# A new order of all engines' turns in the graph stage of a graph-attention and routed-experts kernel

## The reference

```
n = layernorm(x)
h = n @ W
logits = (h @ a_1)^T + h @ a_2 + (h @ a_12) @ h^T        # 512 x 512 for each graph
e = leaky_relu(logits, 0.2);  e = where(adj > 0, e, -9e15)
x = x + elu(n @ W_1 + (softmax(e) @ n) @ W_2)

r = layernorm(x)
top2 of (r @ gate_w + gate_b), weights by softmax over the two
moe = sum over the two of  weight * (relu(r @ w1[e] + b1[e]) @ w2[e] + b2[e])
x = x + layernorm(r + moe) * gamma + beta
```

## Time and profile before

| | |
|---|---|
| three runs | 584.31, 584.80, 587.56 us; median 584.80 |
| profiled execution | 585.1 us, span 583.4 us |
| PE busy | 439.3 us (75%) |
| DVE busy | 368.1 us (63%) |
| POOL busy | 365.4 us (63%) |
| ACT busy | 331.4 us (57%) |

### The profile page before, as it was taken

How to read it: one execution, slowest core, us unless ns; L and a number is a source line. 1 busy time by engine, 2 the same in 40 slices (tenths; PEclk the granted TensorE clock), 3 DMA queues, 4 the chain that set the end, 5 groups by cost and what they waited for, 6 DMA issues and landing times.

```text
span 583.4 us, 12194 instructions
## 1 busy us (share of the span) xinstructions
PE 439.3 (75%) x2959; PEld 352.3 (60%) x2981; DVE 368.1 (63%) x1510; ACT 331.4 (57%) x930; POOL 365.4 (63%) x387
## 2 busy tenths in 40 slices
PE   2589999999999999996311797788798889719650
PEld 2257777777777777775310697788687778603210
DVE  1355888888889888778540365555465556507995
ACT  0487777877777777763200465666466666403453
POOL 1101147777777777557772467777777777735886
PEclk9999999999999999999555899999999999958995
DMA  8622333343333443311162567667667667337852
GB/s 253 208 90 92 91 110 123 102 103 101 126 102 125 124 128 105 114 38 38 46 126 71 162 201 222 193 198 217 204 185 223 198 173 228 106 113 243 260 160 90
DMA packets 89156, 84.45 MB, mean 145 GB/s; under 512 B 11192, under 2 KB 75616, under 8 KB 88960
## 3 DMA queue, kind: packets, MB, share of 16 engines
q1 hardware_dynamic: 76560, 62.64, 38.2%
q0 software_dynamic: 8704, 16.93, 8.5%
q10 hardware_dynamic: 3824, 4.11, 2.5%
HBM read 61.39 MB, written 23.28 MB: 145 GB/s over the span
## 4 chain that ended last, share of the span: by engine, by line
DVE 30%; PE 19%; SPq 18%; issue 13%; POOL 8%; DMA 5%; ACT 4%; ACTq 1%; DVEq 1%; POOLq 0%
SPq L364 7%; SPq L362 7%; PE bank L686 4%; DVE prob L891 4%; DVE bn L875 4%; POOL final_rstd L477 4%; SPq L263 3%; POOL expert_bins L428 3%; DVE final_var L1120 3%; DVE no_edge L869 2%; DMA xg<-expert_bins 2%; PE bank L803 2%; DVE x_sb L920 2%; PE bank L810 2%; DVE z L908 2%
## 5 line engine op out<-in xcount | busy, mean ns | idle before, releaser
L469 POOL DMA_INDIRECT expert_results<-y,xg x144 | 143.1, 994 | 62.8 <-issue 32.5
L428 POOL DMA_INDIRECT expert_bins<-row_out,slots x128 | 135.3, 1057 | 42.6 <-issue 30.8
L629 ACT ACTIVATE hidT<-bank,b_cols 128x128 f32<-128x128 f32 x288 | 90.4, 364 | 54.7 <-PE bank L803 47.0
L1086 DVE TENSOR_TENSOR y<-bank,b_all 128x128 f32<-128x128 f32 x144 | 41.9, 291 | 98.8 <-PE bank L810 93.3
L803 PE MATMUL bank<-xgT,w_cur 128*128 128x128 f32 x576 | 89.8, 279 | 9.3 <-ACT xgT L622 5.3
L810 PE MATMUL bank<-w_sb,hidT 128*128 x576 | 89.4, 278 | 1.3 <-ACT hidT L629 1.3
L803 PEld LDWEIGHTS bank<-xgT,w_cur 128*128 128x128 f32 x576 | 77.2, 195 | 10.6 <-ACT xgT L622 6.1
L810 PEld LDWEIGHTS bank<-w_sb,hidT 128*128 128x128 f32 x576 | 75.5, 191 | 1.9 <-issue 1.9
L694 PEld LDWEIGHTS bank<-vh,probT 128*128 128x128 f32 x512 | 64.1, 191 | 20.4 <-issue 13.9
L686 PE MATMUL bank<-featT,qT 128*128 128x512 f32 x128 | 67.1, 606 | 8.9 <-DVE no_edge L869 6.1
L694 PE MATMUL bank<-vh,probT 128*128 128x128 f32 x512 | 68.7, 278 | 3.6 <-DVE probT L899 2.8
(11 more groups left out here) (139 smaller groups left out, 774.0 us busy)
## 6 DMA issues: line engine op xcount, KB each, us to landing
w_cur<-in_L_ffn_w_dram SPq DMA_DIRECT2D x144, 128.0 KB
adj_sb<-in_adj_dram SPq DMA_DIRECT2D x16, 1024.0 KB
xg<-expert_bins SPq DMA_DIRECT2D x144, 65.0 KB
yy<-expert_results SPq DMA_DIRECT2D x16, 512.0 KB, 4.4
x_sb<-in_x_dram SPq DMA_DIRECT2D x16, 256.0 KB
out_dram<-x_sb SPq DMA_DIRECT2D x16, 256.0 KB, 2.3
expert_results<-y,xg POOLq DMA_INDIRECT x144
expert_bins<-row_out,slots POOLq DMA_INDIRECT x128, 3.3
```

What stands on the lines that cost most here:

```text
L428: nc.gpsimd.indirect_dma_start(bins, bass.IndirectOffsetOnAxis(ap=slots[:, r, i, j:j + 1], axis=0), row_out[:, r, j, i, :], None).then_inc ...
L469: nc.gpsimd.indirect_dma_start(results, bass.IndirectOffsetOnAxis(ap=xg[:, t % XS, D:D + 1].bitcast(U32), axis=0), y[:, t % XS, :], None, ...
L629: r = nc.scalar.activation(hidT[:, t % NB, c * P:(c + 1) * P], hidden_of(t, c), ACT.Relu, bias=b1_cols[:, bass.ds(e * FC + c, 1)])
L1086: V.tensor_tensor(y[:, v, :], out_psum(t), b2_all[:, bass.ds(e * D, D)], ALU.add).then_inc(s_biased, 1)
```

## The change

All four bodies of the graph stage get a new order. Elu and row statistics now belong to graph k - 1, rows, logits, gate, ranks and slots to k - 2. Tile 0 of a graph is scattered in turn k - 2 and tiles 1 to 3 at the start of turn k - 3. The turns run from -3 to 17 (POOL to 18), before from -2 to 18 (POOL to 19). What the order needs in buffers and waits:

- `no_edge` has two buffers, and `mask(k + 1)` stands early in turn k, behind the first score tile.
- `features_products(k)` stands at the end of PE's turn and first waits until the features and queries of graph k + 1 have left the PSUM banks that it writes.
- ACT makes all four copies of the transposed probabilities, and it makes the gate weights, as 1 + tanh and 1 - tanh of half the gap, in place of four small steps on DVE.
- POOL's scatters have no waits on score or probability tiles any more.
- SP is written out graph by graph. The adjacency and x loads no longer wait for x to land; the late weights are issued by SP in turns 2 to 4, not by ACT at the start.
- In the setup the first four weights have their own semaphore, ACT copies the PSUM results, and the statistics of graph 0 run beside it. The b1 transpose moves behind the graph stage.
- At the seam SP issues the first twelve `w1` loads and reads the row table before it waits for the bins.
- `YB`, the result tiles that are loaded ahead in the last loop, goes from 4 to 5.

The core of the diff (of each body's order a line or two; the rows below show the order itself):

```diff
-            no_edge = graph_only.enter_context(nc.sbuf_tensor("no_edge", [P, TPG, N], BF16))
+            no_edge = graph_only.enter_context(nc.sbuf_tensor("no_edge", [P, 2, TPG, N], BF16))
...
-        def turns(body, after=3):
-            for k in range(-2, G + after):
-                body(k, k % 2, k // 2)
+        def turns(body, after=2):
+
+            for k in range(-3, G + after):
+                body(k)
...
+            def load_x(g):
+                sp.dma_start(xg_of(g), x_v[g]).then_inc(s_x[g % 3], 16)
...
+                wait_for(sp, s_mask, g)
+                sp.dma_start(adj_sb[:, :, :], adj_v[g]).then_inc(s_adj, 16)
+
+            load_x(0)
+            sp.dma_start(a2_sb[:, :], a_2).then_inc(s_first_w, 16)
+            sp.dma_start(a1_sb[:, :], a_1).then_inc(s_first_w, 16)
+            load_adj(0)
+            load_x(1)
+            sp.dma_start(gate_sb[:, :], gate_w).then_inc(s_gate_w, 16)
+            sp.dma_start(gate_bias[:, :], bcast(gate_b, E)).then_inc(s_gate_w, 16)
+            load_x(2)
...
+                if g + 2 < G:
+                    load_x(g + 2)
+                if g == 2:
...
+                if g == 3:
+                    sp.dma_start(w2_sb[:, :].rearrange("p (a d) -> p a d", d=D),
+                                 w2.rearrange("e (c p) d -> p (e c) d", p=P)).then_inc(s_late, 16)
...
+            sp.wait_ge(s_tab_done, 1)
+
+            starts = TileNumbers(sp, first_row_i, PAD_ROW)
+            experts = TileNumbers(sp, expert_i, E - 1)
+
+            def load_w1(t):
+                e = experts.of(t)
+                wait_for(sp, s_mm1, t - WS + 1)
+                sp.dma_start(w1_cur[:, t % WS, :], w1[bass.ds(e, 1)].rearrange("a p f -> p (a f)")).then_inc(s_w1[t % WS], 16)
+
+            for t in range(WS):
+                load_w1(t)
+            starts.fetch(0)
             sp.wait_ge(s_pad, 16 * E)
-            sp.wait_ge(s_tab_done, 1)
             for g in range(G - RB, G):
                 bin_wait(sp, g)
-            starts = TileNumbers(sp, first_row_i, PAD_ROW)
-            experts = TileNumbers(sp, expert_i, E - 1)
...
-                row, e = starts.of(t), experts.of(t)
+                row = starts.of(t)
                 wait_for(sp, s_sc[t % XS], 16 * (t // XS))
                 sp.dma_start(xg[:, t % XS, :], bins[bass.ds(row, P), :]).then_inc(s_xg[t % XS], 16)
-                wait_for(sp, s_mm1, t - WS + 1)
-                sp.dma_start(w1_cur[:, t % WS, :], w1[bass.ds(e, 1)].rearrange("a p f -> p (a f)")).then_inc(s_w1[t % WS], 16)
+                if t >= WS:
+                    load_w1(t)
...
+                if k >= 0 and has(k, -2):
                     rstds(0, k + 3, s_mv1, s_rs1)
-                if has(k, 4):
-                    scatter_row(k - 4, 2, 0)
                 if has(k, 2):
                     rstds(TPG, k - 1, s_mv2, s_rs2)
-                if has(k, 4):
-                    after_masked(k, 2)
-                    scatter_row(k - 4, 2, 1)
-                    after_masked(k, 3)
-                    scatter_row(k - 4, 3, 0)
-                    after_prob(k, 3)
-                    scatter_row(k - 4, 3, 1)
-            turns(body, 4)
+                if has(k, 3):
+                    for i in range(1, TPG):
+                        for j in range(K):
+                            scatter_row(k - 3, i, j)
+                if has(k, 2):
+                    pool.wait_ge(s_slot, k - 1)
+                    pool.wait_ge(s_row_out, k - 1)
+                    settle(pool)
+                    for j in range(K):
+                        scatter_row(k - 2, 0, j)
...
+            def gate_weights(g):
                 act.wait_ge(s_gap, g + 1)
-                wait_for(act, s_slot, g)
-                nc.scalar.activation(gate_exp[:, :], gap[:, :], ACT.Exp).then_inc(s_gexp, 1)
+                nc.scalar.activation(gate_tanh[:, :], gap[:, :], ACT.Tanh, scale=-0.5).then_inc(s_gtanh, 1)
+                act.wait_ge(s_gtanh, g + 1)
+                for j in range(K):
+                    nc.scalar.activation(row_out[:, g % RB, j, :, D + 1:D + 2].rearrange("p a b -> p (a b)"), gate_tanh[:, :],
+                                         ACT.Identity, bias=ones[:, 0:1], scale=1.0 - 2.0 * j)
...
+                    exps(k, 2)
+                if has(k, 2):
+                    gate_weights(k - 2)
+                    rows_out(k - 2)
+                if has(k, 1):
+                    elu_exp(k - 1)
+                if has(k, 0):
+                    products_copy(k)
                     relu(k, 3)
...
-            pe.wait_ge(s_gnn_w, 16 * 9)
+            pe.wait_ge(s_first_w, 16 * 4)
...
+                    if i == 0:
+                        pe.wait_ge(s_ft_sb, min(k + 2, G))
+                    if i == 2:
+                        pe.wait_ge(s_qt_sb, min(k + 2, G))
...
-                wait_for(pe, s_hv_sb, 2 * g - 1)
+                wait_for(pe, s_hv_sb, 2 * g - 3)
...
-                wait_for(pe, s_hv_sb, 2 * g)
+                wait_for(pe, s_hv_sb, 2 * g - 2)
...
-                wait_for(dve, s_s, k * TPG)
-                V.tensor_scalar(no_edge[:, :, :], adj_sb[:, :, :], 0.0, NEG_INF, ALU.is_le, ALU.mult).then_inc(s_mask, 1)
+                wait_for(dve, s_s, (k - 1) * TPG)
+                V.tensor_scalar(no_edge[:, k % 2, :, :], adj_sb[:, :, :], 0.0, NEG_INF, ALU.is_le, ALU.mult).then_inc(s_mask, 1)
...
+            def inverse_sums(g):
+
+                dve.wait_ge(s_exp, (g + 1) * TPG)
+                V.reciprocal(rinv[:, :], tiles_of(row_sum, g)).then_inc(s_rinv, 1)
...
-                dve.wait_ge(s_gexp, g + 1)
-                V.tensor_scalar(gate_sum[:, :], gate_exp[:, :], 1.0 / K, 1.0 / K, ALU.mult, ALU.add)
...
-                s.did(V.reciprocal(row_out[:, r, 0, :, D + 1:D + 2].rearrange("p a b -> p (a b)"), gate_sum[:, :]))
-                s.wait()
-                V.tensor_tensor(row_out[:, r, 1, :, D + 1:D + 2].rearrange("p a b -> p (a b)"), gate_exp[:, :],
-                                row_out[:, r, 0, :, D + 1:D + 2].rearrange("p a b -> p (a b)"), ALU.mult)
```

More of the change, by code:

```diff
@@ L748, in body @@
                 if has(k, 0):
[L749 removed]
+                    scores(k, 0)
                 if has(k, 1):
@@ L946, in body @@
                 if has(k, 0):
                     scores(k, 0)
-                if has(k, 2):
-                    elu_parts(k - 2, b)
+                if k == 0:
+                    feature_shift(1)
+                    first_stats(2)
+                if has(k, -1):
+                    mask(k + 1)
                 if has(k, 0):
                     scores(k, 1)
+                if has(k, 2):
+                    rows(k - 2)
                 if has(k, -2):
-                    first_stats(k + 2)
@@ L961, in body @@
+                if has(k, 1):
+                    elu_parts(k - 1)
+                    elu_sum(k - 1)
+                if has(k, 0):
                     scores(k, 3)
                 if has(k, 1):
-                    pt_copy(k - 1, 3)
-                if has(k, 3):
-                    slot(k - 3)
-                if has(k, -2):
-                    feature_shift(k + 2)
-                if has(k, -1):
-                    mask(k + 1)
-                if has(k, 2):
-                    rows(k - 2)
+                    stats(k - 1, TPG, s_bn2, s_mv2)
```

333 lines of the change are left out of this document (165 added, 168 removed).

## The result

| | before | after |
|---|---|---|
| median of three runs | 584.80 us | 601.09 us (599.07, 601.09, 603.89) |
| ratio, 95% interval | | 1.027 (1.021 to 1.032) |
| profiled execution, span | 585.1, 583.4 us | 599.07, 597.3 us |
| masks of graphs 4 and 15 begin | 78.05, 249.38 | 67.21, 261.14 |
| slots of graph 15 | 295.43 | 316.70 |

The change makes the kernel slower by 16 us, and the 584.3 forecast (range 568 to 593) was wrong: the profiled execution is 14.8 above it.

The account below looks back on a forecast made before the run. PE's work and DVE's mask were taken to bound the graph stage's turn, POOL's 144 scatters the expert stage. From 585.1 us, first result scatter 1.2 late and expert stage 2.0 shorter gave 584.3 us, range 568 to 593.

Parts of the forecast that it names:

- Start, turns 0 to 2: Setup and first turns: first scores at 17.1, a gain of 8.6 us, then turns of 18.5, 12.9 and 15.6 us.
- PE waits for rows, not for the mask: Steady turns: PE waits 1 to 1.5 us for `row_out` in each turn and no longer for `no_edge`.
- The ring, 16.28: Steady turn: chain of waits through DVE (5.55), PE (5.90, 0.20 to reach ACT) and ACT (4.63), 16.28 us.
- POOL aside as a rival: Steady turn: POOL's two scatters, features' power and rows' power decide, turn 16.9 us, kernel 591.5 us; chance 0.14.
- The ring without POOL: Steady turn: 16.28 us through DVE, PE and ACT, with POOL's power ready 0.4 us before DVE needs it.
- The clock in steady turns: PE's clock falling inside steady turns was listed as a sign that the forecast is wrong.
- Drain and seam: Last full turn to slots of graph 15 42.5 us, then 16.0 to first tile load, 10.9 to first result scatter.
- Expert stage: From the first result scatter on: a lead of twelve weight loads takes 2 us of the gaps, 189.7 to 187.7.

Follow-up runs that it names:

- e8: Changed kernel with `mask(k + 1)` behind score tile 1 on DVE and features' power early on POOL: turn 16.68 us, 1.006 of the kernel before, 585 us chip.
- e5: Changed kernel with ACT's relu of score tile 3 ahead of the two product copies: turn 18.75 us, 1.012 of the kernel before, 667+ us chip.
- the fill: Changed kernel with eight extra identity transposes on PE ahead of its wait for rows: turn 17.20 us, 1.017 of the kernel before, 585 us chip.
- fill of three: Changed kernel with mask behind first statistics, features' power early, relu of tile 3 first, three extra PE transposes: turn 16.60 us, 0.977 of kernel before, 667+ us chip.
- the slow form: Changed kernel with the mask made in place by `scalar_tensor_tensor`, taking 2.29 us: turn 19.73 us, 1.046 of the kernel before, 667+ us chip.
- the mask late: Changed kernel with `mask(k + 1)` moved behind the first statistics on DVE: turns 16.92 and 16.93 us, 0.986 of the kernel before, 667+ us chip.

## Why the prediction was wrong, point by point

- **Start, turns 0 to 2**: right. First scores at 17.40 (forecast 17.1), graph 3's at 63.10 (17.1 + 18.5 + 12.9 + 15.6 = 64.1).
- **PE waits for rows, not for the mask**: right in kind, 2.11 us where 1 to 1.5 was forecast.
- **The ring, 16.28: the step that failed.** I had put POOL aside as a rival because its power would be ready 0.4 us before it was needed; it came 0.63 late. The queue was as I had it (its rival's chain is the measured one), but not its terms: 2.5, 1.5 and 1.5 for two scatters, the features' power and the rows', where the trace has 2.67, 1.36 and 2.30 (168.00 to 174.33). I took the rows' epsilon step and power at 0.25 and 1.04; beside a mask they take up to 1.17 and 2.03. The ring's legs are 6.33 on DVE (169.35 to 175.68, forecast 5.55), 6.19 on PE (to 181.87, forecast 6.10) and 4.67 on ACT (to 186.54, forecast 4.63): 17.19, 0.91 over. Of that 0.70 is the wait for POOL: the rows start at 174.35, and 0.61 behind score tile 1 would be 173.65. The other 0.2 is small terms, 0.08 of it the rows. The first kernel's trace had shown the hold, a scatter of 1.89 beside a mask at 156, where I read only that scatters vary:

```profile
155.98 1.22 DVE L869 TENSOR_SCALAR no_edge<-adj_sb 128x2048 bf16<-128x2048 int32 x1
156.14 1.89 POOL L428 DMA_INDIRECT expert_bins<-row_out,slots  x1 [0.30 <-DVE slots L1022]
```

- **The ring without POOL.** By this trace it is 17.19 - 0.70, about 16.5, an estimate: 0.2 over my 16.28. The run without the wait (e8) has 16.68; its DVE leg is 5.81 (146.71 to 152.52), in which 0.32 is lost at the relu of tile 1, a wait that the forecast's order doesn't have.
- **Hold or queue.** On the 585 us chip no run took them apart, and on the others POOL is hardly waited for. From the trace, as estimates, either repair might do: without the hold of the epsilon step POOL's ring is 17.19 - 0.92 = 16.27, under 16.5; without the features' power ahead of it, the epsilon step could begin behind the row statistics at 171.36, 0.67 earlier, and the power ahead of the mask, where e5 has at most 1.66 for one begun up to 0.4 ahead.
- **The clock in steady turns**: I had named its fall as what would prove me wrong, and priced it at nothing. It cost 4.7 us: 1.5 of turn 3's 19.10 (63.10 to 82.20, forecast 16.3) and 3.2 in turns 13 and 14. By the Trainium skill (TensorE: Matmul & The Clock Gate, What's actually happening) activity releases the clock; the fill, which leaves the ring alone and gives the 4.7 us back, agrees.
- **Drain and seam**: slots of graph 15 follow graph 15's first scores (273.78) by 42.9 (forecast 42.5), the first tile load 17.75 behind (16.0: SP's pads, issued in 4.13, stand ahead of the weights), the first result 9.36 behind that (10.9). Right within 1.8 each, and they cancel.
- **Expert stage**: forecast 2 us gained, measured 2.1.

Sum of the misses: 14.7 at the slots (-1.0 before graph 3, +2.8 in turn 3, +9.3 by the ring and +3.2 by the clock in the next eleven, +0.4 in the drain), +1.75, -1.5, -0.1: 14.8, the whole of it. Without the clock's 4.7 the profiled execution would have been at 594.4, still above the range's 593.

## What to carry to other kernels

Before you let an engine's short step stand in a ring with 0.4 us to spare, look in the trace for that engine's other instructions beside the long ones of its neighbour: here every POOL instruction that began while DVE's mask ran ended only behind it. When a change makes PE stand longer, price what that does to its clock. When you hold a repair against the changed kernel, look first whether the wait that it is to close is there on that chip: here it was there in one turn of eleven. Two repairs are cheap to try: move the long operation to where its engine waits anyway, and give PE something to do in its wait. The second gave back 4.7 us in one kernel, and as a fill of three nothing in another.

## What the runs showed of the hardware that I had not expected

- POOL stands still while DVE runs the mask, if it begins beside it: epsilon step 1.17 (0.25 alone) and 2.22 beside the slow form, power 2.03 (1.04), scatter 1.89 (0.96). Begun ahead of the mask it depends on how far: a power begun 0.02 ahead took 1.31, from 0.30 to 0.65 ahead 1.56 to 1.91 (e5), and 0.89 ahead (171.00) its own 1.04. A scatter beside DVE's elu step took 1.37. The mask itself stays at 1.20 to 1.25.
- On some chips the kernel before takes 14% longer and the changed one 13%; of the 80 us between the changed kernel's two spans (677.4 and 597.3) 65 lie in the expert stage. Its turn is 1.2 us longer there, and PE's results reach DVE up to 2.2 us later behind its records in most turns, and up to 3.5 in some. The granted clock is no full answer: with the mask late it is 1.00 in every steady turn and the ranks are late all the same.
